# Overflow weights copied on chip by ScalarE, and three more pairs of expert weights loaded in the attention's last chunk

## What is computed

```python
xn = layernorm(x)
# attention without softmax: 16 heads of 16, a decay per head, causal
scores = (q @ k.T) * SCALE * gamma ** (i - j)      # 0 where j > i
y = layernorm(scores @ v) * ln_w + ln_b
attn = (y * silu(xn @ wg.T)) @ wo.T
# experts: 32 of them, width 192, 4 per token
top_vals, top_idx = top_k(xn @ router_w.T + router_b, 4)
rw = softmax(top_vals) * 1.8
routed = sum over the 4 of rw * (silu(xn @ gate_w[e].T) * (xn @ up_w[e].T)) @ down_w[e].T
shared = (silu(xn @ sg.T) * (xn @ su.T)) @ sd.T
out = x + attn + routed + shared
```

## Time and profile before

| | us |
|---|---|
| median of 3 runs | 289.6 |
| lowest and highest | 287.49, 293.31 |
| the profiled execution | 287.65 |
| its span, first to last instruction | 285.8 |
| TensorE busy | 218.1 |
| VectorE busy | 137.3 |
| GpSimd busy | 128.1 |
| ScalarE busy | 62.9 |
| from 257 us (last product) to the end of the span | 28.8 |

### The profile page before, as it was taken

One profiled execution on the slowest core, in us unless ns is written; L12 is line 12 of the kernel. 1 busy time (PEld: TensorE's weight loads), 2 busy tenths in 40 slices (PEclk: granted clock), 3 DMA queues, 4 the chain that ended last, 5 costly groups with the idle time before them and its releaser, 6 DMA issues.

```text
span 285.8 us, 4514 instructions
## 1 busy us (share of the span) xinstructions
PE 218.1 (76%) x1586; PEld 154.4 (54%) x1586; DVE 137.3 (48%) x415; ACT 62.9 (22%) x177; POOL 128.1 (45%) x156
## 2 busy tenths in 40 slices
PE   7599879788399989795999685996895999980000
PEld 2477546555266656554887574665672867830000
DVE  2943989998727582825251403140331234330394
ACT  2131321111001111120231313130322133310240
POOL 2044060425707064644157473737374654443471
PEclk9999999999689999996899997999599699997555
DMA  6989999100000002010104899979949981113972
GB/s 178 405 266 349 349 348 350 60 2 1 0 3 1 2 0 57 0 55 0 39 18 119 286 348 354 354 241 326 338 143 274 309 267 61 42 56 91 358 256 92
DMA packets 41335, 48.59 MB, mean 170 GB/s; under 512 B 2837, under 2 KB 38106, under 8 KB 41184
## 3 DMA queue, kind: packets, MB, share of 16 engines
q1 hardware_dynamic: 37424, 38.87, 42.1%
q0 software_dynamic: 3456, 8.92, 9.6%
q10 hardware_dynamic: 432, 0.50, 0.7%
HBM read 41.99 MB, written 6.82 MB: 171 GB/s over the span
## 4 chain that ended last, share of the span: by engine, by line
PE 53%; DVE 16%; POOL 10%; DMA 6%; another core or an unknown queue 5%; issue 5%; ACT 2%; SPq 1%; POOLq 0%; DVEq 0%
PE bank L1269 15%; PE bank L1281 4%; PE bank L1110 4%; DMA w_early<-y_rows 3%; PE bank L1285 3%; PE bank L1126 3%; PE bank L1141 3%; PE bank L1237 3%; PE bank L1249 3%; POOL arena L607 3%; DVE x_sb L1034 2%; PE bank L1294 2%; PE bank L1203 2%; POOL arena L618 2%
## 5 line engine op out<-in xcount | busy, mean ns | idle before, releaser
L635 POOL DMA_INDIRECT y_rows<-y_mem,codes x36 | 36.2, 1007 | 41.3 <-DVE y_mem L940 32.2
L607 POOL TENSOR_SCALAR arena<-arena,cst 128x256 f32<-128x256 f32 x16 | 14.6, 924 | 64.8 <-ACT arena L487 56.6
L932 DVE TENSOR_TENSOR h_mem<-h_mem,bank 128x128 f32<-128x128 f32 x32 | 9.2, 287 | 64.8 <-issue 24.0
L627 POOL DMA_INDIRECT xg_mem<-xn_rows,codes x36 | 35.3, 981 | 10.4 <-issue 9.8
L1269 PE MATMUL bank<-xb_mem,w_early 128*128 128x128 f32 x216 | 29.7, 288 | 9.8 <-DVE h_mem L934 4.5
L1269 PEld LDWEIGHTS bank<-xb_mem,w_early 128*128 128x128 f32 x216 | 27.5, 202 | 10.5 <-issue 6.2
L882 DVE TENSOR_TENSOR arena<-bank,arena 128x512 f32<-128x512 f32 x32 | 20.5, 682 | 11.5 <-PE bank L1141 11.5
L1269 PE MATMUL bank<-xb_mem,arena 128*128 128x128 f32 x168 | 22.6, 294 | 0.2 <-issue 0.2
L1269 PEld LDWEIGHTS bank<-xb_mem,arena 128*128 128x128 f32 x168 | 21.7, 210 | 0.9 <-issue 0.9
L940 DVE COPY y_mem<-bank 128x256 f32<-128x256 f32 x36 | 13.8, 419 | 15.6 <-remote 7.9
L1141 PE MATMUL bank<-arena 32*128 32x256 f32 x128 | 18.1, 400 | 3.2 <-DVE arena L882 3.2
(11 more groups left out here) (156 smaller groups left out, 369.9 us busy)
## 6 DMA issues: line engine op xcount, KB each, us to landing
w_early<-w_exp_dram SPq DMA_DIRECT2D x9, 1152.0 KB, 12.8
w_early<-w_ovf_dram SPq DMA_DIRECT2D x16, 512.0 KB
arena<-w_exp_dram SPq DMA_DIRECT2D x7, 1152.0 KB
w_early<-y_rows SPq DMA_DIRECT2D x8, 512.0 KB, 8.0
x_sb<-x_dram SPq DMA_DIRECT2D x4, 256.0 KB, 5.7
arena<-w_qkvg_dram SPq DMA_DIRECT2D x2, 512.0 KB, 7.7
arena<-decay_dram SPq DMA_DIRECT2D x1, 1024.0 KB, 10.2
xn_rows<-arena SPq DMA_DIRECT2D x2, 512.0 KB, 3.2
```

Source lines behind the costliest of these rows:

```text
L607: nc.gpsimd.tensor_scalar(qeo[:, t % 2, par * KT * P:(par + 1) * KT * P], q, cst[:, C_PM + par:C_PM + par + 1], None, ALU.mult).then_inc(q ...
L627: nc.gpsimd.indirect_dma_start(xg[:, k % RING, :], None, xn_rows, bass.IndirectOffsetOnAxis(ap=codes[:, c, 0:1], axis=0),).then_inc(tok_in ...
L635: nc.gpsimd.indirect_dma_start(y_rows, bass.IndirectOffsetOnAxis(ap=codes[:, c, 1:2], axis=0), ysb[:, k % YRING, :], None, bounds_check=RO ...
```

## The change

- All 16 pairs get a place of their own in one array `w_mem`, of which `w_early` and `arena` are parts. Behind them lies `o_mem`, with room for the weights of one overflow block.
- ScalarE copies an overflow block's weights on chip: for each sub-block it reads the expert number, and copies 128 x 1024 floats from that expert's place in `w_mem` to `o_mem` (`copy_weights`, `copy_static`). The first of a block's four copies stands at the end of step s, one at the start of step s + 1, two between the even and the odd unit of step s + 1. Before the very first it waits for the weights of all 16 pairs. The copies of block b wait until block b - 1 is done.
- SP loads only the 64 KB part of each sub-block, after the block before is done. `w_ovf` is gone.
- The layout of a pair changes so that each expert's 1152 columns stand together; the size of a pair stays 1152 KB. The odd unit's gate and up halves stand in the even unit's order. A block's gate and up product has 384 columns as before, in another order, so that Silu and multiply of a block are two instructions each.
- The arena's arrays are in another order: those that are free first (the normalised tokens, the projection weights, the router's arrays) stand in front. SP loads pairs 9, 10 and 11 there when the last projections (`qk_ps`, `vg_ps`, `sg_ps` at 8) are done, and no longer after the residuals. After the residuals come pairs 12 to 15, pair p once the down product of pair p - 13 is done, the first at once.
- Overflow blocks start at steps 8, 10, 12 and 14. Their down product stands between the even and the odd unit of step s + 2, the transposition of a block's tokens behind it, and VectorE takes a block's result before it multiplies the odd unit. The scatters follow in the order of the results (`SEQ_Y`).

```diff
-EW = KT * MB + D
+XW = KT * MB + D
+EW = XW + P
-PW = 2 * EW + D
+PW = 2 * EW
-OW = KT * 2 * I + 2 * D
+OW = XW + D
-O_BASE = (5, 8, 11, 14)
-O_HOME = (0, 3 * PW, 6 * PW, 0)
-O_FREES = (2, 5, 8, None)
+O_BASE = (8, 10, 12, 14)
...
-        w_early = sb("w_early", [P, EARLY * PW])
-        arena = sb("arena", [P, 21650])
+        w_mem = sb("w_mem", [P, EARLY * PW + 21650])
+        w_early = w_mem[:, 0:EARLY * PW]
+        arena = w_mem[:, EARLY * PW:EARLY * PW + 21650]
+        o_mem = w_mem[:, PAIRS * PW:PAIRS * PW + SUBS * OW]
...
-            def overflow_in(first, home, signal):
+            def overflow_in(first, signal):
 
                 for j in range(SUBS):
                     e = sp.value_load(eid_row[0:1, bass.ds(first + j, 1)], min_val=0, max_val=E - 1)
-                    o = home + j * OW
-                    sp.dma_start(w_early[:, o:o + OW - D].rearrange("p (c d) -> p c d", d=D),
-                                 w_ovf[bass.ds(e * OPIECES, OPIECES)].rearrange("c p d -> p c d")).then_inc(signal, 16)
-                    sp.dma_start(w_early[0:I2, o + OW - D:o + OW], w_ovf2[bass.ds(e * I2, I2), :]).then_inc(signal, 16)
+                    sp.dma_start(o_mem[I2:P, j * OW + XW:(j + 1) * OW], w_ovf2[bass.ds(e * I2, I2), :]).then_inc(signal, 16)
...
             for p in range(EARLY):
                 pair_in(p)
             sp.wait_ge(xn_out, 32)
+            sp.wait_ge(eid_sb, 1)
+            sp.wait_ge(qk_ps, NT)
+            sp.wait_ge(vg_ps, NT)
+            sp.wait_ge(sg_ps, NT)
+            for p in range(EARLY, EARLY + 3):
+                pair_in(p)
             sp.wait_ge(res_sb, NT)
             sp.wait_ge(eid_sb, 1)
             def paced_pair(p):
-                sp.wait_ge(dn_ps, 2 * (p - EARLY + 1))
+                need(sp, dn_ps, 2 * (p - EARLY - 3))
                 pair_in(p)
 
-            for p in range(EARLY, 12):
+            for p in range(EARLY + 3, PAIRS):
                 paced_pair(p)
-            static_overflow(0)
...
+            for j in range(STATIC_O):
+                need(sp, od_ps, j)
+                overflow_in(SUBS * j, wo_in[j])
...
+            def copy_weights(i, j):
+
+                e = act.value_load(eid_row[0:1, bass.ds(i, 1)], min_val=0, max_val=E - 1)
+                return nc.scalar.copy(o_mem[:, j * OW:j * OW + XW], w_mem[:, bass.ds(e * EW, XW)])
+
+            def copy_static(b, j):
+                need(act, od_ps, b)
+                copy_weights(SUBS * b + j, j).then_inc(ow_sb, 1)
 
             def expert_step(s):
                 if s + 1 < PAIRS:
                     take_pair_tokens(s + 1)
-                if s in O_BASE:
-                    take_overflow_tokens(O_BASE.index(s))
-                if 0 < s < PAIRS:
-                    gate_unit(2 * s)
+                if s - 1 in O_BASE:
+                    copy_static(O_BASE.index(s - 1), 1)
                 if s - 2 in O_BASE:
                     act.wait_ge(oht_ps, O_BASE.index(s - 2) + 1)
                     take_overflow_hidden().then_inc(oht_sb, 1)
+                if 0 < s < PAIRS:
+                    gate_unit(2 * s)
+                if s in O_BASE:
+                    take_overflow_tokens(O_BASE.index(s))
+                if s - 1 in O_BASE:
+                    copy_static(O_BASE.index(s - 1), 2)
+                    copy_static(O_BASE.index(s - 1), 3)
                 if s < PAIRS:
                     gate_unit(2 * s + 1)
+                if s in O_BASE:
+                    if s == O_BASE[0]:
+                        act.wait_ge(eid_sb, 1)
+                        for p in range(PAIRS):
+                            act.wait_ge(we_in[p], 16)
+                    copy_static(O_BASE.index(s), 0)
                 if s - 1 in O_BASE:
                     act.wait_ge(og_ps, O_BASE.index(s - 1) + 1)
-                    gate_overflow().then_inc(osil_sb, 1)
+                    gate_overflow(osil_sb)
...
+                if s - 2 in O_BASE and s < PAIRS:
+                    overflow_result(O_BASE.index(s - 2))
                 if s < PAIRS:
                     multiply_unit(2 * s + 1)
...
-                    pe.wait_ge(wo_in[j], 16 * 2 * SUBS)
-                    overflow_gate_up(O_HOME[j]).then_inc(og_ps, 1)
+                    pe.wait_ge(ow_sb, SUBS * (j + 1))
+                    pe.wait_ge(wo_in[j], 16 * SUBS)
+                    overflow_gate_up().then_inc(og_ps, 1)
```

More of the change, by code:

```diff
@@ L121, in token_blocks, with result_order, build @@
     return seq
+def result_order():
+    seq = []
+    for s in range(1, PAIRS + 1):
+        pair, o = [("P", 2 * s - 2), ("P", 2 * s - 1)], [("O", O_BASE.index(s - 2))] if s - 2 in O_BASE else []
+        seq += o + pair if s < PAIRS else pair + o
+    return seq
 SEQ_X = token_blocks()
 AT = {b: k for k, b in enumerate(SEQ_X)}
-COLUMN = [n if kind == "P" else E + n for kind, n in SEQ_X]
+SEQ_Y = result_order()
+Y_AT = {b: k for k, b in enumerate(SEQ_Y)}
+SENT = [sum(k % YRING == w for k in range(len(SEQ_Y))) for w in range(YRING)]
 X_ORDER = [b for b in SEQ_X if b[0] == "O" or b[1] % 2 == 0]
 X_AT = {b: k for k, b in enumerate(X_ORDER)}
-def build(nc, x, consts, decay, w_router, w_qkvg, w_out, w_sgu, w_sd1, w_sd2, lnwb, rbias, w_exp, w_ovf, w_ovf2, xn_rows, y_rows, out):
+def build(nc, x, consts, decay, w_router, w_qkvg, w_out, w_sgu, w_sd1, w_sd2, lnwb, rbias, w_exp, w_ovf2, xn_rows, y_rows, out):
     with ExitStack() as ctx:
@@ L241, in build @@
         eid = early(1)
+        assert used[0] >= 3 * PW
+        vz = early(2, H * CT)
+        dec = early(H * P)
+        st = early(H * P)
+        xn = st.rearrange("p (t d) -> p t d", t=NT)
+        wo = early(KT, D)
+        wsd1 = early(D)
+        lnw = early(D)
+        lnb = early(D)
+        qk = early(2, 4 * P)
+        qeo = early(2, 2 * KT * P)
+        qd = early(2, KT * P)
+        v = early(2, D)
+        wsd2 = early(D)
+        stats = early(NT, 6)
+        mv = early(NT, 2)
+        rstd = early(NT)
+        var = early(NT)
+        newton = early(NT)
+        half_v = early(NT)
+        gate = early(3, D)
+        ktok = early(D)
+        state = early(KT * P)
+        pmask = early(KT * P)
+        ystats = early(6)
+        ymv = early(2)
+        yrstd = early(1)
+        yn = early(2, D)
+        z1 = early(D)
+        z = early(2, D)
+        sgs = early(I)
+        hs = early(2, I)
+        yT = early(KT * P)
+        zT = early(KT * P)
+        hT1 = early(P)
+        hT2 = early(P)
         xg_mem = sb("xg_mem", [P, RING * D])
@@ L575, in later @@
                 nc.scalar.copy(xbO, ps_ot[:, 0:KT * P]).then_inc(l_xb, 1)
+                for j in range(SUBS):
+                    copy_weights(SUBS * STATIC_O + SUBS * q + j, j).then_inc(l_wc, 1)
                 act.wait_ge(l_og, q + 1)
-                gate_overflow().then_inc(l_sil, 1)
+                gate_overflow(l_sil)
                 act.wait_ge(l_ht, q + 1)
@@ L625, in gather @@
                 pool.sem_inc(pool_go, 1)
-                c = COLUMN[k]
+                c = column(SEQ_X[k])
                 nc.gpsimd.indirect_dma_start(
@@ L633, in scatter @@
                 pool.sem_inc(pool_go, 1)
-                c = COLUMN[k]
+                c = column(SEQ_Y[k])
                 nc.gpsimd.indirect_dma_start(
@@ L1011, in later @@
                 for w in range(YRING):
-                    dve.wait_ge(sent[w], 16 * sum(k % YRING == w for k in range(len(SEQ_X))))
+                    dve.wait_ge(sent[w], 16 * SENT[w])
                 nc.vector.tensor_copy(gidx[:, 0:1], codes[:, bass.ds(E + STATIC_O + q, 1), 0])
                 nc.vector.tensor_copy(sidx[:, 0:1], codes[:, bass.ds(E + STATIC_O + q, 1), 1]).then_inc(l_idx, 1)
-                dve.wait_ge(l_sil, q + 1)
-                multiply_overflow().then_inc(l_h, 1)
+                dve.wait_ge(l_sil, 2 * (q + 1))
+                multiply_overflow(l_h)
                 dve.wait_ge(l_od, q + 1)
@@ L1292, in overflow_gate_up @@
                         rows = slice(SUB * j, SUB * (j + 1))
[L1293 to L1295 removed]
+                        o = j * OW + g * MB
+                        last = nc.tensor.matmul(ps_og[rows, 0:MB], xbO[:, g * P + SUB * j:g * P + SUB * (j + 1)],
+                                                o_mem[:, o:o + MB], start=(g == 0), stop=(g == KT - 1),
                                                 skip_group_check=True)
```

175 lines of the change are left out of this document (61 added, 114 removed).

## The result

The kernel after takes 298.44 us (median of 4 runs, 296.09 to 306.68), the kernel before beside it 288.78 (287.49 to 293.31): ratio 1.032, 95% interval 1.018 to 1.047. It is slower, by some 9 us, and the interval leaves out no change. The forecast was 281.0, its range 273 to 294.5: wrong in sign, and outside the range. Some executions of every kernel here run slower throughout, at a lower granted clock; ratios and intervals leave them out, medians and some of the profiles don't. The profiled execution took 296.09 us, its span is 294.2.

A forecast was written before the change was run, and what follows sets the result against it. It took the expert stage to be stalled by streaming weights together with long indirect-DMA runs. 19.2 - 7.6 - 0.5 - 1.5 - 1.0 = 8.6 us less, from the median 289.6, gave 281.0 us, range 273 to 294.5.

The forecast's parts named there:

- it takes both at once, weights and a long run of indirect DMAs: Expert stage: stalls need streaming weights together with a long run of GpSimd's indirect DMAs; chance of this forecast 0.50.
- Gain: 19.2: Steps 5 to 11: with the weight stream ending near 169.5 us, 19.2 us of stalls go and 2.1 stay.
- excess of 21.3 us: Steps 5 to 11 of the kernel before: they took 61.3 us where undisturbed work needs 40.0.
- R: Theory of the follow-up runs: a run of GpSimd's indirect DMAs holds the other engines up, weights or not.
- rival B: Expert stage: indirect DMAs alone cause the stalls, so nothing of the 19.2 us comes; 294.4 us, chance 0.22.
- step 5's stall: Step 5: the stall should end with the weight stream, some 1.5 us after 169.5, 2.5 us sooner.
- rival E: Steps 3 to 5: the early stalls go too, as one stream replaces many short ones; 276.3 us, chance 0.09.
- rival C: Overflow blocks: ScalarE's reads and copies go in turn, waits of 4.0 us a block; 289.4 us, chance 0.12.
- When they are ready: Overflow blocks: the gate and up product waits 1.9 us for ScalarE's weight copies, four times, 7.6 us.
- rival D: TensorE's clock falls behind each of four 4.0 us waits, about 3.4 us more each; 303.0 us, chance 0.07.
- Late waits: ScalarE before its first copy: waiting for 16 pairs' arrivals, all landed earlier, costs 0.5 us.
- GpSimd's pace, 1.5: Steps 5 to 8: two gathers and two scatters take 5.2 us a step against TensorE's 4.77; charged 1.5 us.

The follow-up runs named there:

- the pair with pauses: Kernel before with GpSimd pausing after each scatter, ratio 0.970; kernel after without ScalarE's copies and with the same pause, ratio 0.969.

## Why the prediction was wrong

**The step that failed** is "it takes both at once, weights and a long run of indirect DMAs", and with it "Gain: 19.2". The excess of 21.3 us is in the rows, and it was right to tie it to GpSimd's runs: with fewer gathers most of it came back. But I took the weights as a second condition from two stretches. The one from 20 to 48 us has no indirect DMAs and says nothing against R. The one of steps 12 to 14 has short runs: from 232.8 us 3 DMAs in a row, a gap of 0.9 us, 2 more, later 3, where the long ones have 8. I named that as the weak spot and still gave it 0.50 against 0.22 for rival B, whose mechanism is the right one. The run without copies (0.996, and 31.8 us of unnamed waits against 32.7) shows that taking the weights off leaves the stalls and the time as they were; the pair with pauses (0.970, 0.969) agrees. Only with GpSimd's runs thinned out does a product wait for streamed weights: 2.42 us with the pauses, 3.15 with few gathers, where the step took 6.0 us more.

The prediction's own check failed too: step 5's stall should have ended with the stream, 2.5 us sooner; ScalarE waits 7.0 us there, to 173.57, longer than the 6.1 of before, to 173.45, so rival E's reason falls as well.

**Rival B's figure** was 294.4; measured is 298.4. What it lacks is most of the copies' waits, of which it counted 3.8 where they cost 8.0. Its rule from the Trainium skill ("DMA: Bandwidth & Descriptors", "SWDGE vs HWDGE vs iDMA": each DMA engine takes turns between the queues) fits in its result: taking 8.4 MB off gave nothing back. It doesn't explain the stalls, which stay when there are no weights to take turns with.

**Copies:** 1.04 us each forecast, 1.042 measured; reads run beside them, as the pair of two copies in 1.98 us shows, so rival C's mechanism is wrong, though waits of its size came about. **When they are ready:** 4 x 1.9 = 7.6 was the second mis-sized term: 4.33, 2.92, 2.92 and 1.57, in all 11.7 of waits and 8.0 of time. The working put the first copy into ScalarE's idle time at the end of the step before. It stands there in the queue, but behind a Silu that a stall held up (219.60 above), so the time began to count some 4 us late. The third block's copies stand behind such a Silu as well (237.18, its product done at 233.62). B's remark that "the waits of steps 9 and 11 fall inside stalls" and cost nothing had it backwards: the stall delays the copies, and the wait comes behind it. With the pauses two of the four waits are near the size forecast.

**The clock (rival D):** behind two of the waits TensorE's block product took 2.79 and 1.67 us in place of 1.50, and the down product 2.08 and 2.07 in place of 1.13. From the block product to the end of the step it is 5.71 us at a granted clock of 0.52 (nearly all at the lower level, 1.2 GHz) and 4.71 at 0.64, against 3.13 at the full clock, 2.4 GHz, behind the second wait. D's mechanism is there, at 2.6 us behind the first and 1.6 behind the third, and not four times; the waits of 2.92 at 225 and of 1.57 left the clock full.

**The 64 KB parts:** forecast hidden behind the copies, and so they were; the last had landed 1.0 us before the block's last copy ended. Without the copies they were to cost 0.5; there one product waits 0.70 for such a part, and another 3.12 for which the profile names nothing.

**Pairs 9 to 11 early:** charged 1.0, nothing measured (0.979 against 0.977), and the stretch up to 168 us is the same in both profiles (156.02:168.07 against 156.06:168.18). **Late waits:** charged 0.5. The first block's first copy starts 1.09 us behind the Silu before it, with the 17 waits and a read between, that of the second block 0.07; so ScalarE lost some 1.0 there, and the first block's wait is the longest. What it did to the time no run separates. **GpSimd's pace, 1.5:** not separated by any run.

**The sum, as it came out** (profiles, from the start of step 3 to the end of the span): 138.2 us against 129.7, so 8.4 more. The copies make 8.0 of it, in place of 7.6 charged, and the rest of the change 0.5, in place of 19.2 gained less 3.0 charged. So the copies' price is near the forecast by luck: 11.7 us of waits in place of 7.6, of which 3.8 would have been waits anyway. The term that failed is the gain.

## What to carry to other kernels

Before a transfer is made cheaper, show that something waits for it: in the kernel before no engine's wait in the stage named the weights, and the stalls ended within 2 us of the ends of GpSimd's runs. A wait that the profile gives to nothing it knows is best tested by taking one suspect away at a time; leaving out the gathers took one run. Where GpSimd issues indirect DMAs beside a pipeline of other engines, try a short pause after every second one, a waited-for 1-element instruction: it gave 3% here without touching anything else. After that look again: once GpSimd paces the stage, or no longer does, another transfer can be what is waited for.

## What the runs showed of the hardware

While GpSimd issues indirect DMAs at a pitch of 1.31 us, other engines start late on results of TensorE that its own rows show as done: 4.2 us (215.37 to 219.60) in the profile after, and up to 7.8 in the kernel before, where ScalarE starts at 201.88 on a transposition that ended at 194.10:

```profile
193.44 0.66 PE L1249 MATMUL bank<-cst,xg_mem 128*128 128x128 f32 x4
...
201.88 0.58 ACT L509 COPY xb_mem<-bank 128x512 f32<-128x512 f32 x1 [10.40 <-remote]
```

It is not ScalarE alone: in the same stretch VectorE has an unnamed wait of 7.28 us, and TensorE idles 2.9 us in four pieces between products of its own that wait for nothing the profile shows. It happens in runs of 8, of 6 and of 5 and, with a pause after each fourth, unnamed waits of 20.2 and 11.6 us stay. With a pause of some 0.9 us after each second they shrink to 12.7 and 1.6, of which 7.3 began ahead of the first pause; with one after each they are gone. Leaving weights off doesn't change the sum (31.8 against 32.7 us). What passes between the engines that such a run holds up, no run here shows; it wasn't tried with transfers other than rows of 1 KB for 128 partitions.
